# Adjacency from sorted edges: groups of 32 destinations chained, each starting on the last pair of edge columns of the group ahead

## What is computed

```python
dst = jnp.minimum((1250 * jax.random.uniform(key, (20000,)) ** 2.0).astype(jnp.int32), 9999)
_o = jnp.argsort(dst, stable=True)
src, dst = src[_o], dst[_o]
...
# attention: an edge counts as often as it occurs
s = jax.ops.segment_sum(p, dst, num_segments=N)
out = jax.ops.segment_sum(alpha[:, :, None] * h[src], dst, num_segments=N)
...
# convolution: sums of edge weights
deg = jax.ops.segment_sum(ew, col, num_segments=n) + 1.0
agg = jax.ops.segment_sum(norm[:, None] * x[row], col, num_segments=n)
```

## Time and profile before

| | |
|---|---|
| median of 3 runs | 3277.78 us (3272.39 to 3284.66) |
| profiled execution | 3266.68 us, its span 3265.0 us, mean granted TensorE clock 0.901 |
| adjacency stage | 0 to about 339 us, loop over groups 17 to 334 us |
| L314 matmuls / L308 matmuls | 2380 / 120 |
| L266 source rows / L267 destination rows | 238 / 238 |
| TensorE busy, whole kernel | 2638.0 us (81%) |
| VectorE busy, whole kernel | 2011.9 us (62%) |

### The profile page before, as it was taken

How to read it: one execution, slowest core, us unless ns; L and a number is a source line. 1 busy time by engine, 2 the same in 40 slices (tenths; PEclk the granted TensorE clock), 3 DMA queues, 4 the chain that set the end, 5 groups by cost and what they waited for, 6 DMA issues and landing times. The chain is left out here.

```text
span 3265.0 us, 40521 instructions
## 1 busy us (share of the span) xinstructions
PE 2638.0 (81%) x14722; PEld 2326.2 (71%) x14723; DVE 2011.9 (62%) x2944; ACT 1356.4 (42%) x2205; POOL 353.4 (11%) x309
## 2 busy tenths in 40 slices
PE   6666486978788696897599959959997998999876
PEld 5555386877787586896388946647765776999766
DVE  7665537977787795223655535172598455898654
ACT  1223235656667563111166620031498201777430
POOL 1233012004003000000023302000000000111000
PEclk9998697989898897998699977969999897999978
DMA  0010311110111115322389981023563132344204
GB/s 32 16 31 16 90 39 37 55 45 20 64 40 51 49 56 133 75 45 61 127 241 261 262 180 30 6 71 130 156 134 76 46 96 48 84 95 100 75 15 99
DMA packets 107207, 268.25 MB, mean 82 GB/s; under 512 B 10894, under 2 KB 49280, under 8 KB 105806
## 3 DMA queue, kind: packets, MB, share of 16 engines
q1 hardware_dynamic: 99440, 239.43, 26.8%
q0 software_dynamic: 7616, 26.74, 3.8%
HBM read 195.58 MB, written 66.73 MB: 80 GB/s over the span
## 5 line engine op out<-in xcount | busy, mean ns | idle before, releaser
L844 PE MATMUL ps<-h,e_gat_aggregate 125*125 125x193 f32 x2400 | 409.0, 334 | 89.2 <-DVE e_gat_aggregate L828 73.2
L844 PEld LDWEIGHTS ps<-h,e_gat_aggregate 125*125 125x125 f32 x2400 | 402.4, 192 | 95.8 <-DVE e_gat_aggregate L828 76.8
L790 ACT ACTIVATE e_gat_aggregate<-row_gat_aggregate,from_src 125x1250 f32<-125x1250 f32 x120 | 160.7, 1339 | 166.8 <-PE ps L844 139.4
L826 DVE TENSOR_TENSOR e_gat_aggregate<-e_gat_aggregate 125x1250 f32<-125x1250 f32 x120 | 175.1, 1459 | 87.0 <-DMA gat_bias_gat_aggregate<-in_gat_b 47.4
L103 PE MATMUL ps<-gat_w_pair_gat_scores,x_turned 128*125 128x384 f32 x1080 | 196.7, 345 | 38.8 <-DVE gat_w_pair_gat_scores L702 38.7
L103 PEld LDWEIGHTS ps<-gat_w_pair_gat_scores,x_turned 128*125 128x125 f32 x1080 | 194.7, 191 | 40.6 <-DVE gat_w_pair_gat_scores L702 39.9
L314 PE MATMUL ps<-dst_hot_build_adjacency,src_hot_build_adjacency 125*125 125x128 bf16 x2380 | 184.8, 234 | 45.9 <-DVE dst_hot_build_adjacency L267 45.2
L314 PEld LDWEIGHTS ps<-dst_hot_build_adjacency,src_hot_build_adjacency 125*125 125x125 bf16 x2380 | 168.3, 147 | 71.3 <-DVE dst_hot_build_adjacency L267 58.5
L103 PE MATMUL ps<-w_pair_dense_rows_from,col_dense_rows_from 128*125 128x384 f32 x1080 | 202.7, 345 | 1.8 <-DVE col_dense_rows_from L973 1.8
L266 DVE TENSOR_SCALAR src_hot_build_adjacency<-ode_iota_build_adjacency,_columns_build_adjacency 125x1250 bf16<-125x1250 f16 x238 | 135.4, 569 | 108.5 <-PE ps L314 71.4
L2315 DVE TENSOR_TENSOR ln_home<-p_attend,p_high_attend 125x1254 fp32r<-125x1254 f32 x120 | 179.1, 1505 | 27.9 <-ACT p_high_attend L2301 25.2
(11 more groups left out here) (376 smaller groups left out, 5048.8 us busy)
## 6 DMA issues: line engine op xcount, KB each, us to landing
stock<-in_moe_w SPq DMA_DIRECT2D x34, 1152.0 KB, 6.2
row_gat_aggregate<-r_scratch SPq DMA_DIRECT2D x24, 625.0 KB, 6.4
V_home<-q_scratch SPq DMA_DIRECT2D x44, 312.5 KB, 6.6
ln_home<-q_scratch SPq DMA_DIRECT2D x36, 312.5 KB
ln_home<-k_scratch SPq DMA_DIRECT2D x36, 312.5 KB
rows_dense_rows_from<-node_scratch SPq DMA_DIRECT2D x9, 1080.0 KB
stock<-in_gat_w SPq DMA_DIRECT2D x4, 2304.0 KB, 8.4
q_scratch<-V_home SPq DMA_DIRECT2D x6, 1250.0 KB, 4.6
```

The lines of the kernel that those rows point to most:

```text
L790: a.activation(e[:, n % 3, 0, :], row[0:TP, head % 2, 0, :], ACT.Exp, bias=from_src[:, head, t:t + 1])
L826: v.tensor_tensor(e[:, n % 3, 0, :], e[:, n % 3, 0, :], e[:, n % 3, 1, :], ALU.max).then_inc(p_step, 1)
L844: last = pe.matmul(ps[0:TP, bank(head, d // 2), d % 2 * (C + 1):(d % 2 + 1) * (C + 1)], e[:, n % 3, 0, d * TP:(d + 1) * TP], h[:, t, head, :],
```

## The change

Neighbouring groups meet in one pair: the last pair of a group is the first of the next. The change makes that a rule (`first` of a group is `last` of the one ahead, and every group goes on by at least one pair), which does the following.

- The first visit of a group builds only destination rows; the source rows are still there from the visit before. The first matmul of each bank in it carries `start=True`, so the matmuls with zeros and the zero tile go.
- The bounds of two groups (three pair numbers, a byte each) and two flags share one word, loaded once per two groups. The wait counts follow from 2i + 80 as long as the chain is unbroken. If the chain would skip a needed pair, the flag `broken` makes every group visit all 80 pairs; the edge tables are therefore three times as long (pair numbers may pass 79).
- The tables: no triangle and no prefix sum by TensorE; instead VectorE takes a running maximum over 40 groups in six doubling steps, on one partition, and packs the words.

```diff
-    def window(w, eng):
-        word = eng.value_load(bounds[0:1, bass.ds(w, 1), :].rearrange("a w two -> a (w two)").bitcast(I32), min_val=0,
-                              max_val=2 ** 16 * (NWIN * NP + NP) + NP * NP - 1)
-        return word % 2 ** 16 % NP, word % 2 ** 16 // NP % NP + 1, word // 2 ** 16
+    def window_pair(i, eng):
+        word = eng.value_load(bounds[0:1, bass.ds(i, 1), :].rearrange("a w two -> a (w two)").bitcast(I32), min_val=0,
+                              max_val=2 ** 26 - 1)
+        pairs = [word % 2 ** 8, word // 2 ** 8 % 2 ** 8, word // 2 ** 16 % 2 ** 8]
+        in_order, out_of_order = word // 2 ** 24 % 2, word // 2 ** 25
+        return pairs, 2 * i + in_order * NP + out_of_order * (2 * NP * i)
...
             for k in range(3):
                 for j in range(2):
-                    last = v.tensor_copy(edge[:, k, j, :], ps[0:TP, 0, (2 * k + j) * NP:(2 * k + j + 1) * NP])
+                    last = v.tensor_copy(edge[:, k, j, 0:3 * NP].rearrange("p (r n) -> p r n", n=NP),
+                                         thrice(ps[0:TP, 0, (2 * k + j) * NP:(2 * k + j + 1) * NP]))
...
             for k in range(3):
-                last = v.tensor_copy(value[:, :, :, k + 1], part[:, k])
+                for j in range(2):
+                    last = v.tensor_copy(value[:, j, 0:3 * NP, k + 1].rearrange("p (r n) -> p r n", n=NP), thrice(part[:, k, j]))
...
-            v.wait_ge(s["tri_done"], 1)
-            step(v.tensor_scalar(lohi[:, 1:2], lohi[:, 1:2], 1.0, float(NP), ALU.subtract, ALU.mult))
-            v.tensor_tensor(lohi[:, 1:2], lohi[:, 1:2], lohi[:, 0:1], ALU.add)
...
+            step(v.tensor_tensor(chain[:, 0, here], high, count_up[:], ALU.subtract))
+            step(v.tensor_scalar(chain[:, 0, here], chain[:, 0, here], 1.0, 1.0, ALU.subtract, ALU.max))
+            for n, by in enumerate((1, 2, 4, 8, 16, 32)):
+                step(v.tensor_tensor(chain[:, (n + 1) % 2, here], chain[:, n % 2, here],
+                                     chain[:, n % 2, SHIFT - by:SHIFT - by + NWIN], ALU.max))
...
+            for j in range(2):
+                src_of(j, slice(0, 1))
             with v.Fori(0, NWIN // 2) as i:
+                pairs, base = window_pair(i, v)
                 for odd in range(2):
                     w = 2 * i + odd
-                    first, end, base = window(w, v)
-                    with v.Fori(first, end) as c:
+                    first = pairs[odd]
+                    for j in range(2):
+                        v.wait_ge(hot_free[j], base + odd + first + 1)
+                        dst_of(j, bass.ds(first, 1), w)
+                    with v.Fori(first + 1, pairs[odd + 1] + 1) as c:
                         for j in range(2):
...
+                            v.wait_ge(hot_free[j], base + odd + c + 1)
+                            src_of(j, bass.ds(c, 1))
+                            dst_of(j, bass.ds(c, 1), w)
...
+            def visit(j, odd, opens):
+                for t in range(NT):
+                    last = pe.matmul(ps[0:TP, 3 * odd + t // 4, t % 4 * 128:t % 4 * 128 + 128],
+                                     src_hot[:, j, t * TP:(t + 1) * TP], dst_hot[:, j].rearrange("p k d -> p (k d)"),
+                                     start=opens and t % 4 == 0, stop=False, skip_group_check=True)
+                last.then_inc(hot_free[j], 1)
...
                     pe.wait_ge(s["staged"], w + 1)
-                    for b in range(3):
-                        pe.matmul(ps[0:TP, 3 * odd + b, :], zeros[:, 0:TP], zeros[:], start=True, stop=False,
-                                  skip_group_check=True)
-                    with pe.Fori(first, end) as c:
+                    for j in range(2):
+                        pe.wait_ge(hot_ready[j], base + odd + first + 1)
+                        visit(j, odd, j == 0)
+                    with pe.Fori(first + 1, pairs[odd + 1] + 1) as c:
                         for j in range(2):
-                            pe.wait_ge(hot_ready[j], base + c + 1)
...
+                            pe.wait_ge(hot_ready[j], base + odd + c + 1)
+                            visit(j, odd, False)
```

More of the change, by code:

```diff
@@ L124, in build_adjacency @@
     w31 = ph.sb("window_last", [NWIN, 1])
[L125 removed]
     hit = ph.sb("window_hit", [NWIN, 2, NP])
[L127 to L131 removed]
+    lohi = ph.sb("window_bounds", [NWIN, 2])
+    SHIFT = NWIN - 1
+    chain = ph.sb("window_chain", [1, 2, SHIFT + NWIN])
+    count_up = ph.sb("count_up", [1, NWIN])
+    first_pair = ph.sb("first_pair", [1, NWIN])
+    broken = ph.sb("chain_broken", [1, 2])
+    words = ph.sb("window_words", [1, 3, 3, NWIN // 2])
+    bounds = ph.sb("bounds", [1, NWIN // 2, 2], U16)
+    edge = ph.sb("edge_columns", [TP, 3, 2, 2 ** 8])
     part = ph.sb("weight_parts", [TP, 3, 2, NP])
[L133 removed]
+    value = ph.sb("edge_values", [TP, 2, 2 ** 8, 4])
     half = ph.sb("weight_bf16", [TP, 2, 2, NP], BF16)
@@ L249, in _ @@
-            v.scalar_tensor_tensor(lohi[:, 2:3], ps[0:NWIN, 2, 0:1], float(NP), lohi[:, 0:1], ALU.add, ALU.subtract).then_inc(s["base_ready"], 1)
-            v.wait_ge(s["bounds_turned"], 1)
-            for k in range(2):
-                v.tensor_copy(bounds[0:1, :, k], ps[0:1, 3, k * NWIN:(k + 1) * NWIN]).then_inc(s["tables"], 1)
+            v.sem_inc(s["lohi_ready"], 1)
+            v.wait_ge(s["bounds_turned"], 1)
+            low, high = ps[0:1, 3, 0:NWIN], ps[0:1, 3, NWIN:2 * NWIN]
+            here = slice(SHIFT, SHIFT + NWIN)
@@ new lines, in _ @@
+            step(v.tensor_tensor(chain[:, 1, here], chain[:, 0, here], count_up[:], ALU.add))
+            step(v.tensor_tensor(chain[:, 0, here], first_pair[:], low, ALU.subtract))
+            step(v.tensor_reduce(broken[:, 0:1], chain[:, 0, here], AX.X, ALU.max))
+            step(v.tensor_scalar(broken[:, 0:1], broken[:, 0:1], 0.0, None, ALU.is_gt))
+            last_pair = chain[:, 1, here].rearrange("a (p two) -> a two p", two=2)
+            v.tensor_copy(words[:, 0, 0], first_pair[:].rearrange("a (p two) -> a two p", two=2)[:, 0])
@@ new lines, in _ @@
+            step(v.tensor_copy(words[:, 0, 1:3], last_pair))
+            step(v.tensor_tensor(words[:, 2], words[:, 1], words[:, 0], ALU.subtract))
+            v.tensor_scalar(broken[:, 1:2], broken[:, 0:1], 2.0 ** 8, 2.0 ** 8, ALU.mult, ALU.add)
+            step(v.scalar_tensor_tensor(words[:, 0], words[:, 2], broken[:, 0:1], words[:, 0], ALU.mult, ALU.add))
+            v.scalar_tensor_tensor(bounds[:, :, 0], words[:, 0, 1], 2.0 ** 8, words[:, 0, 0], ALU.mult, ALU.add).then_inc(s["tables"], 1)
@@ L253, in _ @@
+            v.tensor_scalar(bounds[:, :, 1], words[:, 0, 2], broken[:, 1:2], None, ALU.add).then_inc(s["tables"], 1)
             v.wait_ge(s["tables"], 2)
```

52 lines of the change are left out of this document (20 added, 32 removed).

## The result

| | before | after |
|---|---|---|
| median of 6 runs | 3280.52 us (3272.39 to 3284.66) | 3294.56 us (3290.57 to 3301.93) |
| ratio | | 1.0051, 95% interval 1.0036 to 1.0067 |
| profiled execution | 3266.68, span 3265.0 | 3292.42, span 3290.7 |
| granted clock, 17 to 125 us / 125 to 334 us | 1.00 / 0.92 | 0.91 / 0.74 |
| first and last start of the stage's matmuls | 18.5 / 332.6 us | 24.1 / 343.7 us |

The kernel got 14 us slower, where 6.5 us faster was forecast, and lies beyond the range given (3245 to 3288). The two spans differ by 25.7 us, and not all of that is the change: up to the next stage's first TensorE instruction the difference is 11.0.

What follows compares the result with a forecast made beforehand. The adjacency-building stage ends in a barrier, so its gain or loss is the whole's. Terms -9.9 - 5.5 + 2.1 + 3.8 + 3 = -6.5 us gave 3260.2 profiled, 3271.3 as median; range 3245 to 3288.

Steps and rivals of the forecast that it cites:

- the clock's term: TensorE's clock in the adjacency stage: a few more groups hit by the lower level, +3 us (-3 to +19).
- rival B: Late sparse groups: the clock falls more often, all 28 groups from 12 on hit, +18 us, total 3286; chance 0.16.
- odd lead: Odd groups, last matmul of the group ahead to first true matmul: 0.5 us (0.4 to 0.8), before 1.75.
- odd group, full clock: Odd group with two visits: ends at 5.18 us instead of 5.70, paced by VectorE and GpSimd taking turns.
- even lead: Even groups, last matmul of the group ahead to first true matmul: 1.85 us (1.5 to 2.4), before 2.14.
- even group, full clock: Even group with two visits: ends at 5.73 us instead of 6.05, about -0.3 (0 to -0.4).
- 19 even groups: Even groups 2 to 38 in the loop: a gain together of -5.5 us.
- group 39, at full clock: The last group gets a second visit, of columns that add nothing: 5.2 us instead of 3.08, +2.1.
- prologue: Tables and bounds ahead of the loop: wider copies and more dependent steps, +3.8 us (+2.2 to +5.6).
- A: Inside groups, GpSimd gets in VectorE's way less: up to about -44 us, halfway -25, total 3253; chance 0.27.
- C: Inside groups, GpSimd keeps the port to each sum's end: no group gain, +9 us, total 3287; chance 0.05.
- D: Chain breaks or word misread, every group visits 80 pairs: 3080 visits more, milliseconds; chance under 0.01.

Runs made afterwards that it cites:

- e12_before_again: The kernel before, unchanged, run once more for its trace; its stage took 357.7 us, with a late clock of 0.91.
- e6_before_fill: The kernel before plus four (even groups) or three (odd) matmuls of zeros ahead of the address word's load; 3274.91 us, ratio 0.9993.
- e2_fill: The changed kernel plus filler matmuls of zeros, six per even group's start and two behind each group's first visit; 3269.38 us, ratio 0.9969.
- e8_no_sums: e2_fill without GpSimd's two sums per group, the matrix of weights held constant at 0.5; 3237.86 us, ratio 0.9874.
- e4_src_rebuilt: The changed kernel, with VectorE building the source rows in each group's first visit again; 3291.68 us, ratio 1.0051.
- e3_open_only: The kernel before without the matmuls with zeros, the first visit's matmuls opening the banks, the last group visiting one pair more; 3301.44 us, ratio 1.0070.
- e7_tables_spread: e2_fill with the six value copies moved from VectorE to ScalarE and the memset of ones to GpSimd; 3261.06 us, ratio 0.9945.
- e10_all: e7_tables_spread with ScalarE also copying the source and destination columns from PSUM; 3263.72 us, ratio 0.9948.

## Why the prediction was wrong

**The step that failed is the clock's term, +3.** I took each group against the shortest time that the same group has in any trace of its kind (before, e12_before_again, e6_before_fill; changed kernel and its versions with fillers). By that the lower level cost the changed kernel 24.1 us in groups 1 to 39 and the kernel before 8.8: +15.3, not +3, and +16.0 in the second pair of traces. I had the place (sparse groups late in the stage) and the mechanism as rival B with a chance of 0.16, and its price of 1.0 us per hit group is near what was measured (6.96 against 6.0 even, 6.53 against 5.22 odd).

Too small was the number of groups: a few more than ten in the forecast, 29 with a granted clock under 1.00 in the trace, against 10 in the kernel before. Of the ten even groups with two visits three were hit before (6.76 to 6.92) and all ten are now (6.39 to 6.97 us by the read-out's starts, in e2_fill eight of them 5.96 to 6.08 and two 6.67 and 6.68), four of the ten odd ones with two visits are (5.65 to 6.54 against 5.21 to 5.25), and larger groups early in the stage are as well: numbers 1 and 2, with six and five visits, take 0.8 and 1.1 us longer than in e2_fill, numbers 4, 6, 10 and 12 0.5 to 1.4, where rival B began at group 12.

What I weighed against it, that the clock comes back at once, holds for the kernel before, where each stretch at the lower level ends within one group. In the changed kernel it does not: from 252.9 to 280.2 us, through groups 26 to 29, the granted clock is 0.50 all the time, and where it comes back it mostly falls again in the next even group.

The row for a better weight stood there: the earlier trace rows has 1.00 where most groups had four visits and more, 0.92 where they had two or three, and the edit takes 120 of the longest matmuls out of both. I counted them as 0.69 us of path each group and not as what kept TensorE's clock up. The granted clock over the whole loop was 0.95 before and 0.78 after; with levels of 1.00 and 0.50 that is, as an estimate, some 30 and 140 us at the lower one. The Trainium skill (TensorE: Matmul & The Clock Gate, A second HAM failure mode) tells of short stops between groups of matmuls that make the gate oscillate. This case's traces agree with it, and they give the size: 0.74 and 0.70 without the clearing, 0.96 with fillers.

**The other terms**, in the order of the sum:

| term | predicted | measured | from |
|---|---|---|---|
| odd lead | 0.5 us | 0.51 | after |
| odd group, full clock | 5.18 | 5.21 to 5.25 | after, e2_fill |
| even lead | 1.85 | 1.95 to 2.02 | after |
| even group, full clock | 5.73 | 5.96 to 6.08 | e2_fill |
| 19 odd groups | -9.9 | -9.1 (19 x (5.70 - 5.22)) | before, e2_fill |
| 19 even groups | -5.5 | about -0.4 (19 x (6.06 - 6.04)) | before, e2_fill |
| group 39, at full clock | +2.1 | +2.1 (5.21 - 3.07) | e2_fill |
| prologue | +3.8 | +5.6 (24.1 - 18.5) | before, after |
| groups 9, 17, 25, 33 | not seen | -2.6 (0.60 + 0.77 + 0.69 + 0.53) | e6_before_fill |
| clock | +3 | +15.3 | group by group, as above |

The measured ones add up to -9.1 - 0.4 + 2.1 + 5.6 - 2.6 + 15.3 = +10.9, against 11.0 and 11.7 in the two pairs of traces. The term for the clock makes 12.3 us of the miss, the even groups 5.1, the prologue 1.8, the odd groups 0.8; the line not seen took 2.6 back. (The -5.5 for the even groups is also a small slip of its own: 19 times the 0.32 worked out above it is -6.1.)

The line that I had not seen: in the kernel before every eighth group is longer than its like, at full clock too (e6_before_fill: 17, 25 and 33 take 6.42, 6.34 and 6.18 instead of 5.65, and 9 takes 8.13 instead of 7.53). TensorE's idle time ahead of the clearing is 1.74 us in groups 9, 17 and 25 of the kernel before and 2.15 in group 33, instead of 1.06. The trace shows where it goes, in the load of the address word by TensorE's queue (group 33, then the stretch around it):

```profile
L152 PEldq TENSOR_LOAD <-bounds_build_adjacency x1: 1387/1387/1387, 292.6 to 292.6; - x1
```

```profile
292.00:294.40 2.40, 0.28 (x5) 0.14 (x3) 1.36 (x4) 1.36 (x3) 0.51 (x2) 1.00 0.91 194
```

The load took 1.39 us there and 0.95 to 0.98 in groups 9, 17 and 25, instead of the median's 0.30. Each time SyncE had issued the store of a block of the matrix in the group ahead (at 290.1 us for group 33), and the DMA engines were busy for 0.91 of the stretch shown. The changed kernel loads no word in its odd groups, and none of its loads in the loop behind the first one lasts over 0.38 us; groups 17, 25 and 33 take 5.21 to 5.22 there like the other odd ones. That the store slows the load is read from these coincidences, in the four traces whose groups load a word each; no run was made without the stores.

The odd group was read rightly: lock, order of turns and end to 0.04 us. In the even group the order of turns was as drawn too (source row, second sum, destination row), but all of it came a quarter of a microsecond late: the lead is 2.0 instead of 1.85 (2.06 in e2_fill), the source row comes at T+3.00 instead of 2.75, the second twenty matmuls start at T+4.46 instead of 4.22 and end at 5.97 instead of 5.73. That quarter was nearly the whole gain of about 0.3 us in each of nineteen groups. In the prologue the copies into `value` were sized from rows that ran at another rate: three copies of 160 columns had taken 0.58, six of 240 took 2.69.

**The rivals.** A, GpSimd gets less in the way: no, the turns were as drawn; e8_no_sums shows that without the sums it would have been 4.01 and 5.4. B: yes. Its own sign, a clock under 0.85 late in the stage, came, and its price was nearly right: +18 for all late groups where +15.3 was measured. That the stage lost 11.0 us and not B's 8.5 is the even groups and the prologue. C, the lock holds to the end of each sum: no, the odd group would have been 5.74. D: no, 2400 matmuls. That the spared source rows are worth nothing alone held (e4_src_rebuilt). The median that the forecast was made for, 3277.78 us from three runs, became 3280.52 with three more; the miss does not hang on these 2.7 us.

## What to carry to other kernels

Before you remove matmuls from an engine that is busy in bursts, look at the granted clock of that stretch: work that looks idle may be what keeps the clock up, and taking it off the path can cost more than it gives (e3_open_only: 28 us more for 17 us less path). If the clock is below 1.00 in a stretch where TensorE waits, try matmuls for nothing into a free bank, placed where it waits anyway; here 200 of them gave 21.7 us of a 320 us loop. And when two engines shut each other out, as VectorE and GpSimd do here, lay out the turns from rows before believing a shorter lead: the gain is what is left when the turns are over.

## What the runs showed of the hardware that was not expected

The clock fell without any long stop. In the two groups of the changed kernel shown above, TensorE stands still for 0.51, 0.63, 1.12, 2.00 and 0.17 us; in e2_fill's even group the fillers leave 0.60 ahead of the load and 0.60 ahead of the second visit. The clock of the late stretch was 0.74 without them and 0.96 with them. The visits at the lower level took 2.39 us instead of 1.36 for twenty matmuls of 128 columns.

ScalarE loaded its table once per pair of groups in the kernel before and after (20 loads of 1.28 us); in e7_tables_spread and e10_all, where ScalarE had made a copy ahead of the loop, it did not load one in the loop. The loads lay beside other work, so nothing is claimed for them.
